# A transformer step on one core: queries and keys of two sequences projected in turned form, and a new order on every engine

## The reference

```
# 1. token mixing: groups of 16 rows become 8
q  = (x^T Wq + bq) / sqrt(192);  k, v = x^T Wkv (+ bias on v)      per group of 16 rows
h  = q + softmax(q k^T) v                                          -> 64 x 128 x 192
# 2. attention over the 128 rows of a sequence: 12 query heads, 3 key/value heads, head size 64
n  = layernorm(h)
q, k, v = n @ Wq, n @ Wk, n @ Wv        # 192 x 768, 192 x 192, 192 x 192
rope(x1, x2) = [x1*cos + x2*sin, -x1*sin + x2*cos]                 on q and k, halves of 32
h  = h + softmax(rope(q) rope(k)^T * scale) v @ Wo
# 3. feed-forward, 192 -> 768 -> 192
h  = h + gelu(layernorm(h) @ W_in^T + b) @ W_out
```

## Time and profile before

| | |
|---|---|
| three runs | 1052.17, 1051.24, 1051.01 us |
| the profiled execution | 1053.71 us, of which 1051.8 us from first to last instruction |
| mean granted TensorE clock | 0.982 of full speed |
| busy of the span | TensorE 998.5 us (95%), VectorE 814.6 (77%), ScalarE 733.9 (70%), GpSimd 435.2 (41%) |
| one iteration in the middle | 31.00 us |

### The profile page before, as it was taken

One profiled execution on the slowest core, in us unless ns is written; L12 is line 12 of the kernel. 1 busy time (PEld: TensorE's weight loads), 2 busy tenths in 40 slices (PEclk: granted clock), 3 DMA queues, 4 the chain that ended last, 5 costly groups with the idle time before them and its releaser, 6 DMA issues. The chain is left out here.

```text
span 1051.8 us, 24498 instructions
## 1 busy us (share of the span) xinstructions
PE 998.5 (95%) x7232; PEld 866.3 (82%) x7232; DVE 814.6 (77%) x2095; ACT 733.9 (70%) x2530; POOL 435.2 (41%) x583
## 2 busy tenths in 40 slices
PE   3689999999999999999999999999999999999987
PEld 2577888888988888888888888888889888888865
DVE  2678888778878877888877888887788787788861
ACT  2456777777776677677777777677867777777761
POOL 0334444443544343454444444434345444434440
PEclk7789999999999999999999999999999999999999
DMA  5134434334434434443433454343444344334331
GB/s 174 43 106 134 133 107 143 117 110 127 147 118 116 138 109 118 136 142 110 130 124 106 125 147 126 108 142 112 118 130 146 116 119 132 111 113 146 115 112 45
DMA packets 139935, 127.49 MB, mean 121 GB/s; under 512 B 30992, under 2 KB 123024, under 8 KB 139920
## 3 DMA queue, kind: packets, MB, share of 16 engines
q1 hardware_dynamic: 137632, 124.16, 39.5%
q10 hardware_dynamic: 2288, 3.15, 0.9%
HBM read 70.63 MB, written 56.62 MB: 121 GB/s over the span
## 5 line engine op out<-in xcount | busy, mean ns | idle before, releaser
L403 POOL TENSOR_TENSOR E<-E,e_rcp 128x512 f32<-128x512 f32 x192 | 198.7, 1042 | 284.7 <-DVE e_rcp L534 281.6
L302 ACT ACTIVATE E<-ring,m_neg 128x128 f32<-128x128 f32 x768 | 272.0, 389 | 56.3 <-DVE m_neg L514 56.3
L395 POOL TENSOR_TENSOR q_tok<-rot_c,rot_s 128x384 f32<-128x384 f32 x128 | 125.8, 1005 | 132.7 <-DVE rot_s L492 132.7
L302 ACT ACTIVATION_READ_ACCUMULATOR E<-ring,m_neg 128x1 f32 x768 | 174.7, 227 | 0.0
L514 DVE TENSOR_REDUCE m_neg<-ring 128x4 f32<-128x512 f32 x192 | 122.7, 681 | 57.0 <-PE ring L710 57.0
L296 ACT COPY qkT<-ring 128x512 f32<-128x512 f32 x128 | 71.9, 588 | 128.3 <-PE ring L689 128.3
L525 DVE STREAM_TRANSPOSE EB<-E 128x512 f32<-128x512 f32 x192 | 134.3, 699 | 17.7 <-POOL E L403 17.7
L834 PE MATMUL ring<-wo_sb,OT 128*128 128x192 f32 x768 | 139.6, 332 | 1.5 <-ACT OT L310 1.5
L697 PE MATMUL bank<-wout_sb,G 128*128 128x192 f32 x768 | 135.4, 326 | 2.8 <-ACT G L369 2.8
L697 PEld LDWEIGHTS bank<-wout_sb,G 128*128 128x128 f32 x768 | 125.4, 190 | 3.4 <-ACT G L369 3.3
L834 PEld LDWEIGHTS ring<-wo_sb,OT 128*128 128x128 f32 x768 | 124.1, 191 | 3.9 <-issue 2.4
(11 more groups left out here) (122 smaller groups left out, 2275.9 us busy)
## 6 DMA issues: line engine op xcount, KB each, us to landing
spill<-EB SPq DMA_DIRECT2D x64, 512.0 KB, 2.7
ET<-spill SPq DMA_DIRECT2D x256, 128.0 KB, 2.8
spill<-EB SPq DMA_DIRECT2D x64, 256.0 KB, 2.1
ET<-spill SPq DMA_DIRECT2D x256, 64.0 KB, 2.3
x_sb<-in_x_dram SPq DMA_DIRECT2D x64, 192.0 KB, 2.5
out_dram<-out_sb SPq DMA_DIRECT2D x64, 96.0 KB, 2.3
x_sb<-in_x_dram SPq DMA_DIRECT2D x64, 64.0 KB, 2.3
w_raw<-in_w_att_dram ACTq DMA_DIRECT2D x2, 576.0 KB, 4.8
```

Source lines behind the costliest of these rows:

```text
L302: last = nc.scalar.activation(E[:, a, s * P:(s + 1) * P], RING[a][:, s * P:(s + 1) * P], ACT.Exp, bias=m_neg[:, a, s:s + 1], accum_out=e_s ...
L395: nc.gpsimd.tensor_tensor(q_tok[:, a, c], rot_c[:, a, c], rot_s[:, a, c], ALU.add).then_inc(q_out, 1)
L403: nc.gpsimd.tensor_tensor(e, e, r, ALU.mult).then_inc(prob_out, 1)
```

## The change

Both sequences of a pair are projected together for queries and keys, with a tile of 128 weight columns as the stationary operand and the turned LayerNorm output of both sequences (256 columns) moving: eight column tiles, five matmuls each, in four groups on two banks. The result has head features on the lanes and tokens along the row, so the transposes, their copies and the key addition go. The weight columns are laid out so that each group of 32 lanes holds 16 features of one half of a head and the 16 that RoPE pairs them with, and VectorE exchanges them with a stream shuffle. The multiplication by the sines moves to GpSimd, behind the shuffle, with the addition, for queries and keys and for each sequence alone. Values are projected in the old form, 256 weight columns moving, and a copy of the second sequence's values is kept. h_cur becomes two tiles, copied one by one. The orders of all engines are new. Cut to its core:

```diff
+NW = DQ + 2 * P + DKV
+PROJ = (3, 0, 1, 2)
+HEAD_ROWS = [16 * r + i + 32 * u for r in range(2) for u in range(2) for i in range(16)]
+SWAP = [(i + 16) % 32 for i in range(32)]
...
-        TOK_S, TOK_AT, TOK_H = B7[:, 0:DP], RING[0][:, 1024:1024 + DP], RING[0][:, 1024:1024 + 2 * D]
-        HIDDEN = (B6[:], RING[0][:, 1024:1536], RING[1][:, 512:1024])
+        TOK_S, TOK_AT, TOK_H = RING[1][:, 512 + DP:1024], B7[:, 0:DP], B7[:, 0:2 * D]
+        HIDDEN = (RING[0][:, 1024:1536], B6[:], RING[1][:, 512:1024])
+        V_MM = RING[0][:, 1024:1536].rearrange("p (a c) -> p a c", a=2)
...
 ScalarE
-                def qk_turned(a):
-                    for b in range(2):
-                        c = slice(512 * b, 512 * (b + 1))
-                        act.wait_ge(qT_mm, 4 * p + 2 * a + b + 1)
-                        nc.scalar.copy(qkT[:, a, c], RING[a][:, c]).then_inc(qT_out, 1)
 new order: warm exp; tok_vq(0), tok_vq(1); t_e, t_a; score_exp(0, 0); t_aT; heads_out(1, p - 1);
            score_exp(0, 1), score_exp(0, 2); HH; score_exp(1, 0..2); XH; heads_out(0, p); gelu
...
 GpSimd
-                def turned_in(a): ...
+                def rotated(a, i, done):
+                    b = PROJ[i]
+                    pool.wait_ge(rot_out, 4 * p + i + 1)
+                    sin = (rope_ks if b == 3 else rope_qs)[:].rearrange("p (o t) -> p o t", o=1).broadcast_to([P, 2, P])
+                    nc.gpsimd.tensor_tensor(rot_s[:, b, :, a], rot_s[:, b, :, a], sin, ALU.mult).then_inc(sin_out, 1)
+                    pool.wait_ge(sin_out, 8 * p + done)
+                    nc.gpsimd.tensor_tensor(qkT[:, b, :, a], rot_c[:, b, :, a], rot_s[:, b, :, a],
+                                            ALU.add).then_inc(q_out, 1)
                 if ffn:
                     rstd2(2 * p - 1, 0)
                 if att:
+                    need(pool, sc_mm, 6 * p)
+                    for i in range(4):
+                        rotated(0, i, i + 1)
+                    for i in range(3):
+                        rotated(1, i, i + 5)
+                    wait_apart(pool, pool_passed, (h2_out, 2 * p - 1), (h_out, p + 1))
+                    nc.gpsimd.tensor_copy(h_cur[0][:], h_next[:, 0, :]).then_inc(h_kept[0], 1)
+                    nc.gpsimd.tensor_copy(h_wait[:], h_next[:, 1, :]).then_inc(h_moved, 1)
+                    probs(0, 0, p)
+                    rotated(1, 3, 8)
+                    probs(0, 1, p)
+                    probs(0, 2, p)
                 if ffn:
                     rstd2(2 * p, 1)
 then ve, rs of tok; h_cur[1] <- h_wait; v_late <- v_tok[:, 1]; h2_kept <- h2; probs(1, 0..2)
...
 VectorE
+                def rotate(i):
+                    b = PROJ[i]
+                    dve.wait_ge(qk_mm, 4 * p + i + 1)
+                    src = RING[0][:, 512 * (i % 2):512 * (i % 2 + 1)]
+                    cos = (rope_kc if b == 3 else rope_qc)[:].rearrange("p (o t) -> p o t", o=1).broadcast_to([P, 4, P])
+                    nc.vector.tensor_tensor(rot_c[:, b].rearrange("p c a t -> p (c a) t"),
+                                            src.rearrange("p (x t) -> p x t", t=P), cos, ALU.mult)
+                    nc.vector.stream_shuffle(rot_s[:, b].rearrange("p c a t -> p (c a t)"), src, SWAP).then_inc(rot_out, 1)
+                def v_out_of_psum():
+                    dve.wait_ge(v_mm, p + 1)
+                    nc.vector.tensor_copy(v_tok[:], V_MM[:, :, V_OF:DP]).then_inc(v_out, 1)
 new order: rotate(0..3); tok queries and keys out of PSUM; v_out_of_psum; normalise(.., hn, 0); t_s, t_neg;
            key_max(0, 0); t_rs; key_max(0, 1..2); sums_inverted(0, 0); blocks_turned(0, 0); sums_inverted(0, 1);
            h_next; its statistics; attention_added(1); blocks_turned(0, 1); sums_inverted(0, 2);
            attention_stats(1); blocks_turned(0, 2); normalise(.., hn, 1); key_max(1, 0..1); HL; ffn_result;
            key_max(1, 2); sums_inverted(1, 0); xn; the rest as before
...
 TensorE
+                def qk_projected(i):
+                    b = PROJ[i]
+                    if i == 0:
+                        pe.wait_ge(XH_out, p + 1)
+                    else:
+                        need(pe, rot_out, 4 * p + i - 1 if i > 1 else 0)
+                    xh, xl = ([t[:, c].rearrange("p a t -> p (a t)") for c in range(2)] for t in (XH, XL))
+                    for half in range(2):
+                        c = slice((2 * b + half) * P, (2 * b + half + 1) * P)
+                        for k, (w, r) in enumerate(((WH1, xh[0]), (WL1, xh[0]), (W2S, xh[1]), (WH1, xl[0]), (W2S, xl[1]))):
+                            if i == 0 and half == 0 and k == 3:
+                                pe.wait_ge(XL_out, p + 1)
+                            last = nc.tensor.matmul(RING[0][:, 512 * (i % 2) + half * DP:512 * (i % 2) + (half + 1) * DP],
+                                                    w[:, c], r, start=(k == 0), stop=(k == 4))
+                    last.then_inc(qk_mm, 1)
+                def v_projected():
+                    for a in range(2):
+                        last = group(V_MM[:, a], [(t[:, k, a], w[:, V_COLS]) for t, k, w in
+                                                  ((XH, 0, WH1), (XH, 0, WL1), (XH, 1, W2S), (XL, 0, WH1), (XL, 1, W2S))])
+                    last.then_inc(v_mm, 1)
                 def scores(a):
-                    pe.wait_ge(qT_out, 4 * p + 2 * a + 2)
-                    pe.wait_ge(v_out, 2 * p + a + 1)
+                    pe.wait_ge(q_out, 8 * p + 4 * a + 4)
+                    if a == 0:
+                        pe.wait_ge(v_out, p + 1)
+                    elif tok:
+                        pe.wait_ge(s_masked, n + 1)
                     for h in SCORE_ORDER:
+                        if a == 1 and h == 8:
+                            need(pe, h2_out, 2 * p)
 hn_turned still waits for hn_out of both sequences; ffn_first for HH_out, then HL_out
 new order: qk_projected(0), (1); tok_qk; qk_projected(2), (3); tok_vq; v_projected; ffn_second(0), first 2 of 6;
            tok_scores; scores(0); probs_v(1, p - 1); tok_probs_turned; ffn_second(0), last 4; tok_h;
            output(1, p - 1); ffn_second(1), first 4; scores(1); hn_turned; ffn_second(1), last 2; ffn_first;
            x_turned; probs_v(0); output(0)
```

More of the change, by code:

```diff
@@ L353, in step @@
                 if att:
-                    for g in range(NKV):
-                        score_exp(1, g)
-                    heads_out(0, p)
+                    for k in range(NKV):
+                        score_exp(1, k)
                 if tok:
                     act.wait_ge(xT_mm, n + 1)
-                    nc.scalar.copy(XH[:].rearrange("p a c -> p (a c)"), B7[:]).then_inc(XH_out, 1)
+                    nc.scalar.copy(XH[:].rearrange("p c a t -> p (c a t)"), B7[:]).then_inc(XH_out, 1)
                     if isinstance(p, int) and p == -1:
@@ L366, in step @@
                     nc.scalar.activation(warm[:, 0:1], warm[:, 0:1], ACT.Gelu).then_inc(s_warm, 1)
-                    for m in (2 * j + i for j in GELUS for i in range(2)):
+                    for m in range(NM):
                         act.wait_ge(hid_mm, 3 * (p - 1) + m // 2 + 1)
@@ L569, in step @@
                 if att:
-                    key_max(0, (0, 1, 2))
-                    sums_inverted(0, 0, p)
+                    v_out_of_psum()
+                if ffn:
+                    dve.wait_ge(ln2_rs, 2 * p - 1)
+                    need(dve, hT_mm, p - 1)
+                    normalise(h2, mv2, rs2, hn, 0).then_inc(hn_out, 1)
                 if tok:
@@ L693, in ffn_second @@
-                def ffn_second(a, q):
-                    for m in range(NM):
+                def qk_projected(i):
+                    b = PROJ[i]
+                    if i == 0:
+                        pe.wait_ge(XH_out, p + 1)
[10 more added lines that the diff above has]
+                    last.then_inc(qk_mm, 1)
@@ L708, in scores @@
                             pe.wait_ge(low_mm, 2 * p + a + 1)
-                        rows, s, k0 = slice(half * HD, (half + 1) * HD), SLOT[h], DQ + (P if h >= 8 else 0)
-                        last = nc.tensor.matmul(RING[a][:, s * P:(s + 1) * P], qkT[rows, a, t * P:(t + 1) * P],
-                                                qkT[rows, a, k0:k0 + P], start=True, stop=True)
+                        rows, s = slice(half * HD, (half + 1) * HD), SLOT[h]
+                        last = nc.tensor.matmul(RING[a][:, s * P:(s + 1) * P], qkT[rows, t // 2, t % 2, a],
+                                                qkT[rows, 3, h // 8, a], start=True, stop=True)
                         if h in BANK_ENDS:
@@ L844, in step @@
                 if att:
-                    pe.wait_ge(XH_out, p + 1)
-                    pe.wait_ge(XL_out, p + 1)
-                    qkv(0)
+                    qk_projected(0)
+                    qk_projected(1)
                 if tok:
                     tok_qk()
-                if fin:
-                    ffn_second(0, p - 2)
```

(40 more changed lines are left out.)

252 lines of the change are left out of this document (99 added, 153 removed).

## The result

The changed kernel takes 1116.13 us (median of four runs, 1112.17 to 1117.09) against 1051.12 us: a ratio of 1.061, 95% interval 1.058 to 1.064. The forecast was 1094 us, slower, with a range of 1020 to 1118.

What follows compares the result with a forecast made beforehand. TensorE was taken to set the 31.0 us period. Work of 29.2 plus waits of 3.05 gave 32.2, with the port 32.4: +1.4 in 30 iterations and 1 at the ends, 1051 + 43 = 1094 us; range 1020 to 1118.

Steps and rivals of the forecast that it cites:

- TensorE's work: TensorE per iteration: transposes and qkv go, 50 matmuls of 256 columns come at 0.125 us each; 29.2 us if nothing is late.
- GpSimd's pieces: GpSimd's 16 new operations over 2 x 128 columns per iteration: 0.72 us each, 11.5 us together.
- The shuffle: VectorE's exchange of lanes over 512 columns: 0.70 us, as the block transposition; even 1.4 would delay by under 1 us.
- The chain: From tok_scores' end to hn_out through VectorE, ScalarE and GpSimd: 12.1 us, TensorE waiting 1.75 at hn_turned; all waits 3.05.
- The port: VectorE's normalise(hn, 0) held up by GpSimd operations at a shared port: 0.2 us taken, period from 32.2 to 32.4.
- t_s slips by 0.2: VectorE's t_s, next behind normalise(hn, 0), starts later by 0.2 us, from a range of 0 to 1.1.
- The sum: 1.4 us more in each of 30 iterations, +42, and about +1 at the ends; 1051 + 43 = 1094 us.
- The ends: The two partial iterations at the kernel's start and end: about +1 us together.
- The clock: TensorE's clock should stay full; if waits let it fall, the time is above the range; no us were put on it.
- Rival 1: TensorE stays covered, only small waits remain: period 29.8, 1015 us, up to 1042; faster, chance 0.28.
- Rival 2: GpSimd becomes the bound: at 0.85 us an operation period 33.2, 1118 us; slower, chance 0.10.
- Rival 3: The two effects cancel: a chain 1.2 us shorter pays back what the transposes gave; no change, chance 0.04.

Runs made afterwards that it cites:

- e1_chain: Changed kernel with only VectorE's order changed: sums_inverted(0, 2) and the residual's LayerNorm statistics ahead of turning group 1; 1080.15 us, ratio 1.027 to the kernel before.
- e2_norm0: Changed kernel with only normalise(hn, 0) moved on VectorE, from ahead of t_s to behind key_max(0, 1..2); 1096.72 us, ratio 1.042 to the kernel before.
- e5_light: Changed kernel without GpSimd's multiplication by the sines, so the output is not RoPE's; 1094.91 us, ratio 1.040 to the kernel before.
- e3_out: Changed kernel with TensorE's x_turned back between probs_v(0) and output(0), and ScalarE's heads_out(0) ahead of XH; 1113.55 us, ratio 1.060 to the kernel before.
- e4_both: Changed kernel with the edits of e1_chain and e2_norm0 together; 1060.79 us, ratio 1.009 to the kernel before.
- e6_filler: e4_both with TensorE's ffn_second(1) split 2 + 4 instead of 4 + 2; 1068.14 us, ratio 1.016 to the kernel before.

## Why the prediction was right, and what it missed

The direction, the place and the engines of the wait were right. That the time lies in the range is in part luck: 1116 is 2 us below its upper end, and two terms that the sum had at nothing or nearly so, the clock and the ends of the kernel, used most of the room up.

- **TensorE's work.** Forecast 0.75 us more for projections, 29.2 in all. In the changed kernel the projections of queries and keys, with tok_qk between them, go from 527.98 to 534.15, 6.17:

```profile
530.45 0.60 PE L766 MATMUL ring<-bd_qk,x_sb 128*128 128x128 f32 x4
530.89 1.06 PE L770 MATMUL ring<-bd_qk,x_sb 128*128 128x128 f32 x8
531.70 0.37 PE L673 MATMUL ring<-XH,WH 128*128 128x256 f32 x1
...
534.15 0.81 PE L777 MATMUL bank<-x_sb,bd_vqv 128*128 128x384 f32 x2
```

  tok_qk takes 1.25 of that, which leaves 4.92 for 40 matmuls, 0.123 each: as taken. tok_vq and the ten for the values take 2.47 (534.15 to 536.62), less tok_vq's 1.39 of before that is 1.1. So the addition is 0.5, at the lower side. The work as a whole is not smaller than forecast: by the distances between starts, an estimate, all waits of an iteration together are 3.3 of the 32.59, which leaves 29.3.
- **GpSimd's pieces.** Taken 0.72, bounds 0.67 and 1.0; measured 0.735. The nearest row, the old addition, was a good guide. The estimate of 0.56 from the 4497 ns of the Trainium skill's "GPSIMD Engine Reference", section "Elementwise — side-by-side cycle accounting", was too low: the trace does not agree with scaling that figure down to 256 columns. GpSimd's load was given as near 21.6, though 13.59 less four additions and 11.5 more is 21.1; measured 21.8 in an iteration, with the new copies of h_next and the values (0.35 each) that the sum doesn't name.
- **The shuffle.** Taken 0.70; measured 0.735, with a mask load of 0.01 to 0.02 that hides. It was covered, as said.
- **The chain.** Forecast waits at tok_h, hn_turned, output(0) of 0.2, 1.75 and 0.33; measured under 0.1 (the matmul's row has none), 1.58 and 0.34. At tok_probs_turned the schedule had TensorE on time (the list of waits has a 0.1 that stands at no place); measured 0.43. The place, the engines in it and the order of the links are shown by the trace and by e1_chain, which changes only VectorE's order.
- **The port.** I took 0.2 us of a range of 0 to 1.1. The step "t_s slips by 0.2" was mis-sized: e2_norm0 puts it at 0.60. Both halves took over twice their time, as the Trainium skill's "SBUF — State Buffer", section "Who interferes with whom", has it of an operation in a two-port mode against a GpSimd operation; here each ended just behind the GpSimd operation beside it (538.44 against 538.34, 539.19 against 539.13). The trace agrees with that rule for both halves. It does not agree for hn's second half at 550.57, which GpSimd's rs on 2 columns, begun before it and 0.71 long, did not hold up. The upper end by that rule, a period of 33.3, was too much: together the halves took 1.49 us (537.61 to 539.10), and 0.88 of that fell in time in which t_s waited for TensorE anyway (the idle time in front of it in e2_norm0). The 0.6 that is left is the loss.
- **The sum.** The forecast's 43 us were thirty iterations of 1.4 and 1 for the ends. Between the profiled executions it is 62.5. Period 32.6 against 32.4: 5.6 us more over the 29 full iterations. Five of them took 1.3 more behind TensorE's clock: 6.6 us. The ends: the first hn comes 6.0 us later (85.94 to 91.98), the thirtieth distance grew by 1.7 (29.16 to 30.88), the one behind it by 3.4 (21.69 to 25.07), the rest is 1.7 shorter: 9.4 against 2.4 forecast, 7.0 more. These three make 19.2 of the 22 us from 1094 to 1116; nearly all the rest is the profiled execution of the kernel before, 2.6 above its median. The ends were the largest term that I did not work out. What makes them long is not settled: e5_light takes 6.3 us out of the last two distances, e3_out 3.4 (30.42 and 22.13), and no run was made for the first.
- **The clock.** I had said that it should stay full, and that the time would be above the range if the waits let it fall. It fell five times in full iterations, and the time is inside the range: both parts of that sign were wrong, and a term of 6.6 us was put at nothing without a reason.
- **The rivals.** Rival 1 needed a chain under 10.9 us from tok_scores' end to hn_out. It is 12.5 (538.38 to 550.88), against 12.1 forecast. Rival 2 is excluded by e5_light for the full iterations. Rival 3, a period as before, came only when both links were taken out (e4_both).

## What to carry to other kernels

Removing work from the fullest engine pays only as far as the other engines still answer in time; follow, for every place where that engine waits for a result, the whole queue of each engine in the chain and write down its length from rows, as was done here to 0.2 us in 32 (helped by single waits that missed by 0.1 to 0.4 in both directions). Work out the first and the last iterations too: here they cost more than the error in the period. A wait on an in-order engine delays all that is queued behind it, so the first edit to try is the order there: a few calls moved on VectorE alone gave back 55 of the 65 us. Filler on the waiting engine helps only outside a distance that others set, and moving it can make another engine's queue late.

## What the runs showed of the hardware

- TensorE's granted clock fell to half (1.2 GHz) for some 3 us in some iterations, starting 1 to 2 us behind the end of a wait in which TensorE had done nothing for 1.58 us; each time costs 1.3 us. Between 100 and 1020 us it was seen in every kernel with a wait of 1.58 at hn_turned (five longer distances in the changed kernel, four each in e2_norm0 and e3_out, seven in e5_light, there every fourth iteration), while the kernels with 0.67, 0.68, 0.99 or 1.28 there kept the full clock. Shorter waits are not safe by that: behind the first transposes of hn the clock also fell after a wait of 1.31 in e4_both and of 1.29 in e6_filler, but not after 1.30 in e1_chain. Why one iteration and not the next was not tried.
- VectorE's tensor_scalar over 192 and over 64 columns took 0.83 and 0.82 us beside GpSimd operations over 256 columns that followed each other, and 0.38 and 0.31 beside one on 2 columns of 0.71 us.
- A GpSimd operation over 2 x 128 columns takes 0.735 us, over 384 columns, in the kernel before, 1.005, over 512 with one input repeated 1.05.
- The block transposition and the stream shuffle from PSUM, both over 512 float32 columns, take 0.70 and 0.735 us.
